# Two-layer decoder on one core: six of sixteen x tiles projected inside self-attention, cross-attention products in half and quarter arrays, and a new exchange of the largest |x|

## The reference, cut to what matters

```python
def quat_norm(q, eps=1e-06):
    r, i, j, k = jnp.split(q, 4, axis=-1)
    n = jnp.sqrt(r * r + i * i + j * j + k * k + eps)
    return jnp.concatenate([r / n, i / n, j / n, k / n], axis=-1)
...
q = quat_norm(quat_linear(x, qW, qb))      # layer 0 self-attention, 16 heads of 16
k = quat_norm(quat_linear(x, kW, kb))
v = quat_linear(x, vW, vb)
scores = jnp.einsum('bthd,bshd->bhts', q_, k_) * scale
scores = scores + jnp.mean(jnp.sin(J[:T])) * 0.1
attn = jax.nn.softmax(scores, axis=-1)
out = jnp.einsum('bhts,bshd->bthd', attn, v_).reshape(B, T, D)
...
# layer 1 cross-attention: 16 heads of 16, 77 context rows per batch
attn = softmax(q k^T / 4);  out = attn v;  out @ Wo.T + bo
...
# layer 1 feed-forward with quantised activations
def act_qdq(x):
    scale = jnp.maximum(jnp.max(jnp.abs(x)) / qmax, 1e-12)
    return jnp.clip(jnp.round(x / scale), -qmax - 1.0, qmax) * scale
x = act_qdq(x);  up = act_qdq(x @ w_up.T);  gate = act_qdq(x @ w_gate.T)
```

## Time and profile before

| quantity | value |
|---|---|
| median of 3 runs | 869.48 us (868.73 to 871.26) |
| the profiled execution's own time | 869.56 us |
| its span, first to last instruction | 867.8 us |
| outside the span | 1.76 us |
| mean granted TensorE clock | 0.958 |
| busy: PE / PEld / DVE / ACT / POOL | 752.1 / 431.9 / 522.2 / 552.0 / 191.5 us |
| costliest line | L535, ACT, 256 exponentials, 235.4 us |

### The profile page before, as it was taken

The page is one execution under the profiler, slowest core; times in us unless marked ns, Lnnn a source line. Parts: engine busy times, 40 slices in busy tenths (PEclk is TensorE's granted clock), DMA queues, the critical chain, the costliest instruction groups (busy, mean ns, idle before and its releaser), DMA issues.

```text
span 867.8 us, 10805 instructions
## 1 busy us (share of the span) xinstructions
PE 752.1 (87%) x3849; PEld 431.9 (50%) x3849; DVE 522.2 (60%) x1088; ACT 552.0 (64%) x941; POOL 191.5 (22%) x214
## 2 busy tenths in 40 slices
PE   4986899999999988998799998679899979994397
PEld 2642111111111137977688886445656844441286
DVE  4899332322111129779524648869967567898886
ACT  3656999999999962324132152575777433598991
POOL 1778000000000003215003202385543200000013
PEclk9996999999999999999899999799999989998599
DMA  7210213131364410302055000002100000000002
GB/s 198 100 25 1 49 33 78 26 85 25 87 202 66 118 47 1 97 1 98 1 194 193 1 1 1 0 0 74 37 0 2 1 1 0 1 0 0 0 25 73
DMA packets 57373, 42.13 MB, mean 49 GB/s; under 512 B 36866, under 2 KB 54120, under 8 KB 57192
## 3 DMA queue, kind: packets, MB, share of 16 engines
q1 hardware_dynamic: 57176, 41.31, 17.2%
q10 hardware_dynamic: 144, 0.13, 0.1%
HBM read 28.59 MB, written 4.46 MB: 38 GB/s over the span
## 4 chain that ended last, share of the span: by engine, by line
PE 38%; ACT 30%; DVE 21%; issue 7%; DMA 1%; SPq 1%; POOL 1%; DVEq 0%; POOLq 0%; ACTq 0%
ACT arena L535 24%; PE banks L1786 5%; PE banks L1778 5%; PE banks L1579 5%; PE banks L1567 5%; PE banks L1679 3%; PE banks L1651 2%; DVE arena L894 2%; DVE arena L902 2%; DVE arena L1186 2%; PE banks L1476 2%; DVE arena L790 2%; ACT arena L712 1%; ACT arena L698 1%; PE banks L1599 1%
## 5 line engine op out<-in xcount | busy, mean ns | idle before, releaser
L535 ACT ACTIVATE arena<-banks 128x1024 f32<-128x1024 f32 x256 | 235.4, 1094 | 3.1 <-PE banks L1349 3.0
L1349 PE MATMUL banks<-arena 128*32 128x512 f32 x1024 | 138.1, 611 | 2.2 <-ACT arena L535 0.8
L855 DVE COPY arena<-banks 128x512 f32<-128x512 f32 x16 | 11.1, 692 | 180.6 <-PE banks L1349 180.6
L1335 PE MATMUL banks<-arena 64*128 64x512 f16 x512 | 99.4, 390 | 23.1 <-ACT arena L535 9.4
L359 POOL TENSOR_SCALAR arena<-arena 128x2 f32<-128x2 f32 (+1 forms) x38 | 12.7, 334 | 462.2 <-DVE arena L897 462.2
L1335 PEld LDWEIGHTS banks<-arena 64*128 64x128 f16 x512 | 24.7, 93 | 166.8 <-ACT arena L535 154.4
L1778 PE MATMUL banks<-arena 128*128 128x512 f32 x192 | 85.9, 609 | 3.9 <-DVE arena L1197 3.7
L626 ACT ACTIVATE arena<-banks,arena 128x77 f32<-128x77 f32 x256 | 58.9, 363 | 22.2 <-DVE arena L1110 22.1
L1786 PE MATMUL banks<-arena 128*128 128x256 f32 x192 | 44.5, 397 | 26.6 <-ACT arena L733 26.6
L1579 PE MATMUL banks<-arena 128*128 128x256 f32 x256 | 58.2, 389 | 5.8 <-DVEq L1032 5.8
L1778 PEld LDWEIGHTS banks<-arena 128*128 128x128 f32 x192 | 37.3, 196 | 51.8 <-issue 48.8
(11 more groups left out here) (215 smaller groups left out, 1314.5 us busy)
## 6 DMA issues: line engine op xcount, KB each, us to landing
arena<-in_L_ffn_w SPq DMA_DIRECT2D x16, 1024.0 KB, 7.5
w_kept<-arena SPq DMA_DIRECT2D x3, 768.0 KB, 3.6
arena<-w_kept SPq DMA_DIRECT2D x3, 768.0 KB, 4.4
arena<-in_x SPq DMA_DIRECT2D x4, 512.0 KB, 8.7
out_x<-arena SPq DMA_DIRECT2D x3, 512.0 KB, 2.9
arena<-in_L_ffn_b SPq DMA_DIRECT2D x1, 1024.0 KB, 9.1
arena<-in_L_ffn_w_gate SPq DMA_DIRECT2D x1, 768.0 KB, 7.2
arena<-in_L_ffn_w_up SPq DMA_DIRECT2D x1, 768.0 KB, 8.9
```

Source lines behind the costliest of these rows:

```text
L535: act.activation(PT[kt % 2][:, half], PS[:, 2 * (n % 3):2 * (n % 3) + 2, :], ACT.Exp, scale=DH ** -0.5 / QK_UP ** 2).then_inc(sem("exp_don ...
L1335: mm = pe.matmul(bank(2 * (n % 3) + h), KT[u % 2][64 * h:64 * h + 64, P * kt:P * kt + P], QT[u % 2][64 * h:64 * h + 64, 512 * half:512 * h ...
L1349: mm = pe.matmul(PS[32 * j:32 * j + 32, 6, :], VS[w][:, kt, h, :], PT[kt % 2][:, half, h, :], start=(kt == 0), stop=(kt == TB - 1))
```

## The change

The diff makes these edits, which are given here by stage.

1. Head. The loop covers `HT = 10` tiles only. POOL no longer adds the v bias; it is scaled once and folded into `stage` (one instruction becomes two with two operands each). For tiles 0 to 6 the low part moves from DVE to POOL (two instructions of 128x256 each); for tiles 7 to 9 DVE makes the high and the low part. `stage(0)` moves to t = 10. PE starts the scores after 10 tiles.
2. Units 0 to 5 of self-attention. Tile 10+u is projected in unit u through bank 7: a 256-column f32 matmul behind `values` at each kt from 0 to 5, and two transposes ahead of the last `values` of units 0 to 4. DVE adds the biases, copies v and the turned x, and normalises the tile before (a bit-trick seed and three Newton steps, 9 small instructions, then product and f16 copy). POOL squares, adds, and makes the low part. `stage(8)` waits for all tiles.
3. Cross-attention. `xa_scores` contracts over the 64 rows that hold non-zero keys, so its two matmuls use different row halves of the array. The five value chunks are reordered (`PAIRED`); chunks c = 0 to 3 become pairs of 64-column matmuls that write different partitions, the fifth (104 rows) stays whole. `vmask` is cut in two parts: four selects on POOL in place of two.
4. Quantised feed-forward. The first exchange goes over PE and DVE (`x_top`) in place of POOL; `largest` is called for the other four alone. The quantisation of x in group 0 is cut in two by k, and the first |up| of 2048 columns in 512 and 1536; one scalar product is moved ahead of a wait.

```diff
@@ constants
+HT = 10
+LATE = T - HT
+CHUNK = (0, P, 2 * P, 2 * P + 2 * REST, 3 * P + 2 * REST)
+ROWS = (P, P, 2 * REST, P, P)
+PAIRED = (0, 3, 1, 4, 2)
+X_TOP_AT = 3
+UI_FIRST = (slice(0, 512), slice(512, T * P))
@@ POOL, head
-            for t in range(T):
-                pool.wait_ge(sem("v_evac"), t + 1)
-                v = VV[:, NP * (t // TB):NP * (t // TB) + NP, t % TB, :]
-                pool.tensor_tensor(v, v, bq4[:, 2].rearrange("p (u w) -> p u w", u=NP), ALU.add).then_inc(sem("v_biased"), 1)
+            for t in range(HT):
...
+                if t >= 3:
+                    low_part(t - 3)
+            for i in range(LATE + 1):
+                if i < LATE:
+                    late_norm(i)
+                if i >= 1:
+                    late_low(i - 1)
@@ POOL, masks and exchanges
-            pool.affine_select(out=vmask, in_=vmask, compare_op=ALU.is_ge, fill=0.0, base=0,
...
+            for n, (i0, i1) in enumerate(((0, 3), (3, NC5))):
+                pool.affine_select(out=vmask[:, i0:i1], ...
-            largest(0, 0)
-            largest(1, 3)
...
+            largest(0, 3)
@@ DVE, self-attention
+            def late_biased(i):
+                t = HT + i
+                dve.wait_ge(sem("qk_mm"), t + 1)
+                dve.tensor_tensor(qk_sb[t % 3]..., bank(7), bq4[:, 0:2]..., ALU.add).then_inc(sem("qk_biased"), 1)
+            def late_qn(i):
...
+                for _ in range(3):
+                    link(dve.scalar_tensor_tensor(w, y, -0.5, y, ALU.mult, ALU.mult))
+                    link(dve.tensor_tensor(w, w, v, ALU.mult))
+                    link(dve.scalar_tensor_tensor(y, w, 1.5, y, ALU.add, ALU.mult))
...
             def attn_unit(u):
                 if u + 1 < UN:
                     stage(u + 1)
                 if 1 <= u <= 9:
                     quantised((u - 1) // 3, (u - 1) % 3)
+                if u < LATE:
+                    late_biased(u)
+                if 1 <= u <= LATE:
+                    late_qn(u - 1)
+                if u < LATE:
+                    late_v(u)
+                if u + 1 < LATE:
+                    late_x(u + 1)
@@ DVE, largest |x|
-            dve.tensor_reduce(sc[:, 0:1], xmax, AX.X, ALU.max).then_inc(sem("amax"), 1)
-            dve.wait_ge(sem("gmax"), 1)
+            dve.tensor_reduce(sc[:, 0:1], xmax, AX.X, ALU.max).then_inc(sem("x_amax"), 1)
+            dve.memset(ones_row[0:1, :], 1.0)
+            dve.wait_ge(sem("x_amax_row"), 1)
+            dve.tensor_reduce(sc[0:1, 38:39], bank(2)[0:1, 0:P], AX.X, ALU.max).then_inc(sem("x_top"), 1)
+            dve.wait_ge(sem("x_top_all"), 1)
+            link(dve.tensor_copy(sc[:, 10:11], bank(3)[:, 0:1]))
@@ PE, self-attention
             def attn_unit(u):
                 for kt in range(TB):
                     for n in range(2 * (TB * u + kt) + 3, 2 * (TB * u + kt) + 5):
                         if n < 2 * TB * UN:
                             scores(n)
+                    if kt == TB - 1 and u + 1 < LATE:
+                        late_turn(u + 1)
                     values(u, kt)
+                    if u < LATE:
+                        late_project(u, kt)
@@ PE, cross-attention
-                    mm = pe.matmul(PS[:, 2 * (n % 2) + q, 0:4 * LC], qTx[g % 2][:, k, P * j:P * j + P],
-                                   Kbd[:, k, g // 2, 4 * q:4 * q + 4, :]...
+                    rows = slice(64 * q, 64 * q + 64)
+                    mm = pe.matmul(PS[:, 2 * (n % 2) + q, 0:4 * LC], qTx[g % 2][rows, k, P * j:P * j + P],
+                                   Kbd[rows, k, g // 2, 4 * q:4 * q + 4, :]...
...
+                    if c < 4:
+                        cut = slice(64 * (c % 2), 64 * (c % 2) + 64)
+                        pe.matmul(PS[cut, b0 + k, cols], Vx[:, g // 2, k, i, cut], PTx[g % 2][:, NC5 * k + c, cols], start=(c < 2), stop=False)
@@ PE, largest |x|
+            def x_top():
+                pe.wait_ge(sem("x_amax"), 1)
+                pe.transpose(bank(2)[0:1, 0:P], sc[:, 0:1], ident).then_inc(sem("x_amax_row"), 1)
+                pe.wait_ge(sem("x_top"), 1)
+                pe.matmul(bank(3)[:, 0:1], ones_row[0:1, :], sc[0:1, 38:39], start=True, stop=True).then_inc(sem("x_top_all"), 1)
```

More of the change, by code:

```diff
@@ L517, in _ @@
             x_evac(0)
[L518 to L519 removed]
+            for t in range(HT + 1):
+                if t + 1 < HT:
                     x_evac(t + 1)
[L521 removed]
+                if 3 <= t < HT:
                     high(t - 3)
[L523 removed]
+                if t < HT:
                     square(t)
                     v_evac(t)
[L526 removed]
+                if t >= 1:
                     norm(t - 1)
@@ L711, in _ @@
                     act.wait_ge(sem("f_u_scale"), 1)
-                act.activation(ui[:, c, :], UF[:, c, :], ACT.Abs, scale=sc[:, 26:27]).then_inc(sem("f_ui"), 1)
+                for part in UI_FIRST if c == 0 else (slice(0, T * P),):
+                    act.activation(ui[:, c, part], UF[:, c, part], ACT.Abs, scale=sc[:, 26:27]).then_inc(sem("f_ui"), 1)
                 if c == IC - 3:
@@ L830, in stage @@
                     dve.wait_ge(sem("pv_done"), TB * (u - 1))
-                dve.tensor_scalar(VS[w][:, :, :, 0:DH], VV[:, u].rearrange("p t (h d) -> p t h d", h=2), ec, None, ALU.mult).then_inc(sem("vs"), 1)
+                for h in range(2):
+                    bias = bq4[:, 2, 2 * DH * (u % NP) + DH * h:2 * DH * (u % NP) + DH * h + DH]
+                    ins = dve.scalar_tensor_tensor(VS[w][:, :, h, 0:DH], VV[:, u, :, DH * h:DH * h + DH], ec,
+                                                   bias[:, None, :].to_broadcast([P, TB, DH]), ALU.mult, ALU.add)
+                ins.then_inc(sem("vs"), 1)
             def quantised(n, part):
@@ L994, in _ @@
             for n, i in enumerate((4, 0, 1, 2, 3)):
-                rows = LASTR if i == NC5 - 1 else P
+                rows = ROWS[i]
                 dve.wait_ge(sem("l1_v_mm"), n + 1)
@@ L1351, in values, with late_turn, late_project @@
                 mm.then_inc(sem("pv_done"), 1)
+            def late_turn(i):
+                t = HT + i
+                if t % 4 == 0 or i == 0:
+                    pe.wait_ge(sem(f"x_in{t // 4}"), 16)
+                if i >= 1:
+                    pe.wait_ge(sem("v_evac"), t)
+                for k in range(KD):
+                    mm = pe.transpose(bank(7)[:, P * k:P * k + P], X[:, t, P * k:P * k + P], ident)
+                mm.then_inc(sem("x_tr"), 1)
+            def late_project(i, kt):
+                t = HT + i
+                x = xTs[t % 2]
+                if kt == 0:
+                    pe.wait_ge(sem("xT"), t + 1)
+                if kt < 4:
+                    m, k = kt // 2, kt % 2
+                    mm = pe.matmul(bank(7)[:, D * m:D * m + D], x[:, k], Wq4[:, k, m, :], start=(k == 0), stop=(k == KD - 1))
+                    if kt == 3:
+                        mm.then_inc(sem("qk_mm"), 1)
+                if kt in (4, 5):
+                    k = kt - 4
+                    if k == 0:
+                        pe.wait_ge(sem("qk_biased"), t + 1)
+                    mm = pe.matmul(bank(7)[:, 0:D], x[:, k], Wq4[:, k, 2, :], start=(k == 0), stop=(k == KD - 1))
+                    if k == KD - 1:
+                        mm.then_inc(sem("v_mm"), 1)
             def attn_unit(u):
@@ L1363, in _ @@
             pe.wait_ge(sem("quat_w_upper"), 1)
-            for t in range(T):
-                if t + 1 < T:
+            for t in range(HT):
+                if t + 1 < HT:
                     x_turn(t + 1)
@@ L1660, in p_turn @@
                 e = Ex[n % 4].rearrange("p h l -> p (h l)")
-                for c in range(NC5):
-                    rows = LASTR if c == NC5 - 1 else P
-                    mm = pe.transpose(PS[0:rows, 4 + c // 4, P * (c % 4):P * (c % 4) + P], e[:, P * c:P * c + rows], ident)
+                for c, i in enumerate(PAIRED):
+                    mm = pe.transpose(PS[0:ROWS[i], 4 + c // 4, P * (c % 4):P * (c % 4) + P], e[:, CHUNK[i]:CHUNK[i] + ROWS[i]], ident)
                 mm.then_inc(sem("xa_ptr"), 1)
```

163 lines of the change are left out of this document (114 added, 49 removed).

## The result

The changed kernel takes 860.17 us (median of 4 runs, 858.76 to 861.56) against 869.17 for the kernel before on the same chip: ratio 0.9885, 95% interval 0.9857 to 0.9913: 9.0 us faster by the medians, 10.0 by the ratio. The forecast was 846.8, with 836 to 858 as its range: the sign is right, the size isn't, and the time lies outside the range. The profiled execution took 861.56 (span 859.8), the longest of the four. In the experiments, one of e4's six executions took 1366.03 us with a granted clock of 0.828 over its span, and is left out of e4's median and ratio.

A forecast was written before the change was run, and what follows sets the result against it. It took DVE to bound the head, ACT self-attention, DVE then PE cross-attention. Terms -16.9 - 0.3 + 9.5 + 0.6 - 9.5 - 6.2 = -22.8 from 869.56 gave 846.8 us, range 836 to 858.

The forecast's parts named there:

- Head: Before self-attention: first exponential at about 61.0 instead of 77.9 us, -16.9 us, bounds -15 to -18.5.
- Start of the units: Unit 0 of self-attention: the 3.3 us lost there before become 3.0, bounds 2 to 5; sum -0.3 us.
- late tiles: Self-attention units 0 to 5: added products, transposes and DVE stalls cost +9.5 us, bounds 3 and 15.
- Rival B: Late units: DVE and POOL hold each other up, bank 7 late; 8 to 12 us more, 856 us; chance 0.15.
- Masks: Two more selects on POOL and their waits, on the chain: +0.6 us, bounds 0 and 0.8.
- Cross-attention: Row-half scores and paired values shorten PE's work, not all arriving: -9.5 us, bounds -4 and -13.
- Largest |x|: Exchange before the gate products: first product 3.3 us earlier, PE's clock stays up; -6.2 us, bounds -3 and -6.5.
- D: First exchange: its POOL cost only moves to the reduction behind the gate maximum, +4.2 us, 851 us; chance 0.12.
- C: Units 0 to 5 and cross-attention: array shape changes are dear, gain gone at 0.36 us each; chance 0.04.
- A: Units 0 to 5: late tiles cost little, 3 to 5 us; with cross-attention at -12, 838 to 841 us; chance 0.22.

The follow-up runs named there:

- e4: Changed kernel with only the largest |x| put back to the reduction over partitions on GpSimd: 864.50 us, ratio 0.9931 to the kernel before.
- e6: Changed kernel with HT = 12, four tiles late instead of six: 860.29 us, ratio 0.9870 to the kernel before.
- e2: Changed kernel with VectorE doing late_qn ahead of late_biased and the quantised piece behind it: 853.22 us, ratio 0.9821 to the kernel before.
- e7: Changed kernel with the six late products of a unit in pairs behind steps 0, 2 and 4: 856.14 us, ratio 0.9842 to the kernel before.
- e9: Changed kernel with both late_qn ahead of late_biased and the late products in pairs: 856.83 us, ratio 0.9830 to the kernel before.
- e1: Changed kernel with all 16 tiles of x in the head and none late: 859.56 us, ratio 0.9883 to the kernel before.
- e11: Changed kernel with unused transposes filling TensorE's waits at cross-attention steps 16 and 27: 859.34 us, ratio 0.9859 to the kernel before.
- e3: Changed kernel with cross-attention's scores on all 128 rows again, paired values kept: 860.43 us, ratio 0.9890 to the kernel before.
- e8: Changed kernel with the six late tiles' work spread over units 0 to 6: 863.09 us, ratio 0.9904 to the kernel before.

## Why the prediction was wrong, step by step

**Head, -16.9: right in size.** -15.1 in the profiled execution, which is a late one. In the ten traces with ten tiles in the head (e6 has twelve) the first exponential is at 59.3 to 63.9, on average 61.2; the forecast was 61.0. The spread comes from the head's start: the first projections took 3.67 us from 21.75 on here, in e2 1.98 from 20.14. What set the pace up to tile 9 was PE, busy 21.88 of the 22.00 us from 27 to 49 with DVE at 18.61. The last tile follows the one before it by 2.8 us, which the forecast had for PE. POOL's work on a tile stayed at 2.9 to 3.0 us, under 3.3.

**Start of the units, -0.3, and late tiles, +9.5: the step that failed.** Together 9.2 forecast, 15.2 measured. Two terms were too small. "I take 0.53 for the late matmul, bounds 0.43 and 0.63": it is 0.63, the upper bound, since a visit of the whole array between strips and halves costs 0.20 us (e7), where I had added one change's 0.10; 36 products, 3.6 us. The visit's own price did not decide this alone: in e9 the six steps with products cost just what the forecast had (12.38 us, 12.36 forecast), and the unit still took 16.70 instead of 16.1, because PE then loses 0.44 us in the seventh step, waiting for ACT, a wait that the forecast's unit does not have. The excess that I had read between strips and halves is not the price of going to the whole array. And DVE's stall: "0.4 us in units 1 to 4", measured 0.97 each, 2.3 us more in sum; e2, which removes it, gave 3.8 us over these four units. With these, 9.2 + 3.6 + 2.3 = 15.1; unit 0 alone wanders by 1.5 us from trace to trace. The range for the late tiles, 3 to 15, did reach that far; the total's range did not reach 860, because it needed this bound and the next one at once. Rival B named the second mechanism (POOL and DVE hold each other up, the late turn waits for DVE), and its size, 8 to 12 us, was far too large: `late_qn` took 6.1 instead of 4.6 us.

**Masks, +0.6: right.** +0.5 at the experts.

**Cross-attention, -9.5: failed.** Measured -2.6. Its last part was right: the half values took 15.25 us from the first to the group turn before and 13.08 after, -2.2 as forecast. What failed is "So not all arrives: three quarters, 6.8". PE's own work shrank about as priced (a score pair 0.72 us from start to start instead of 1.04), but from the experts to the half values nothing arrived: 251.65 us before, 251.24 after. PE's gain turned into waits for ACT, 12.0 us instead of 5.7, and into slower work: behind three of these waits after step 6 the clock fell to 1.2 GHz, where it had not fallen before, and at two of the three places nothing hid the slower work. Where it stayed up at these two (e1, e4) the whole stretch is 3 us shorter. Why it falls in one trace and not in another, behind the same waits, stays open. I had written that PE was the bound from 627 on; it was, by a margin that the edit used up at once. The 1.8 us that are lost by step 6 divide so: 0.5 from the masks, still there when the conv projection starts just ahead of step 6 (581.42 and 581.88); 1.6 from that projection (3.56 and 5.16 us to the scores that follow it), which ran at the lower clock, behind a wait of 1.83 instead of 1.46 us; and 0.3 back from the shorter score pair. Not every trace with the changed code has this fall (e6, e9 and e11 keep the clock there); e3 keeps it too.

**Largest |x|, -6.2: right in mechanism, a little large: -5.9 from the group turn to the span's end.** From the group turn to the first gate product 11.6 us before and 8.8 after, -2.8 (3.3 forecast), and from there to the first down product 2.5 less (2.9). The granted clock is 1.00 as forecast.

**Rivals.** D is refuted: POOL's first reduction follows DVE's by 0.1 us (743.28, DVE's ends at 743.14), and no idle time is put down to issue. C is refuted in size, with the price of a visit at 0.20, not 0.36 or more a change; but its direction, that changes of shape eat the gain, is what happened in units 0 to 5. A, with units of 15.1 us, is refuted by every late unit.

## What to carry to other kernels

Moving work off a head into a stage that another engine paces pays only up to that engine's slack: here TensorE had 2.5 us a unit to spare and got 3.8 us of products, 0.4 of transposes and 0.4 of waiting for a copy, so that the six tiles cost as much as they saved (e1, e6). Then look for the queue ahead of the copy that frees the shared bank: putting `late_qn` first on VectorE (e2) brought 5.6 us, the whole move none. And when the bound engine has little margin over the next, do not count three quarters of what you take from it: count what is left of the next engine's chain, and reckon with more of TensorE's work at the lower clock behind the new waits.

## What the hardware showed that I had not expected

- A full-array product between 32-column strips and 64-row halves costs 0.20 us more than the product itself, once for one product or for two in a row (0.63 and 1.07 us with 0.43 for each product).
- The same code from `hidden` to the end of cross-attention took 286.3 to 289.8 us from one profiled kernel to the next. Behind a wait of 2.61 us the clock fell in the changed kernel and not in e4, and the same behind one of 1.4 us at step 27.
- Four f16 copies on VectorE took 9.32 instead of 0.62 us beside GpSimd's additions, and 1.71 to 3.74 us of waiting for their transposes followed on TensorE where `stage` of the next unit was late (before, e8, e1).
